# Vision tower on one core: patch sums of the second image half moved behind the first half's value sums, its mean in a product of its own

## Chip, cores, metric

One NeuronCore of a Trainium2 chip. The metric is the device time of one launch in microseconds (us). The kernel before has a median of 334.91 us over 3 runs (334.71 to 335.78).

## What is computed

A small vision tower on 64 images of 3 x 84 x 84, all in float32: a tokenizer, then two layers of delta-rule attention with a gated feed-forward, then a feed-forward with block-wise 4-bit rounding of inputs and weights. The change lies in the tokenizer, which gives 4 window tokens and 1 class token of 256 channels for each image. Cut to what matters:

```python
pe = conv(pixel_values, conv_w, stride 14)            # 6 x 6 patches of 14 x 14, 256 channels
grid = pe in windows of 3 x 3                         # 4 windows an image, 9 patches each
red = mean of the 9 patches                           # one query vector for a window
win = the 9 patches
q = _ln(red) @ la_wq;   k_, v_ = _ln(win) @ la_wkv     # 8 heads of 32
attn = softmax(q . k_ * scale over the 9)
agg = sum over the 9 of attn * v_
local_out = red + agg @ la_proj_w + la_proj_b
```

The kernel carries a mean-free form: the convolution weights are centred over the channels, so its `red` lacks the channel mean. That mean is a linear function of the pixels and is added back where `local_out` is formed.

## The kernel before

**Tiling.** A window is a column. The 256 windows (4 for each of 64 images) are two halves of 128, the "image halves" hf 0 and 1. The pixels lie in six groups g of 384 columns (3 patches x 128 windows): groups 0 to 2 are the first half, 3 to 5 the second. Each group is 5 chunks of 120 pixel rows (`xg`, in the tile `big`). The convolution `conv(g, c)` (L1131) makes patches of 128 channels in PSUM, ScalarE copies them to `pecT` (L336), and keys and values are products of `pecT` with the weights, two patches in a unit `un`; units 0 to 4 are the first half, 5 to 9 the second.

**Order.** Each engine runs its own list, written out by hand, and waits on semaphores (the names in `S[...]`), so an instruction that waits holds all that is behind it on its engine.

- GpSimd (L261 on): `patch_sum(g)` adds the three patches of a group into `xs[:, hf]`, 8 additions of 120 x 640 a half (L280); `square_sum(g)` adds the squares of the two channel chunks (L287). The order is patch sums 0 to 2, square sums 0 to 5, patch sums 3 to 5. Behind them GpSimd waits for `gag_mm`, which comes at about 125 us.
- TensorE (L1114 on): `keys(un)` (L1175), `value(un)` (L1189), `gathered(un)` (L1202), which adds a unit's weighted values into a PSUM sum and raises `acc`; `red_mean` (L1211), which gets the channel mean of all 256 windows from `xs` into PSUM bank 3, 10 products of 256 columns as the profile counts them; `project(hf)` (L1226), the output projection; `stat(hf)` (L1163).
- VectorE (L578 on): `scores(un)` (L698 multiplies the keys in PSUM with the query, L701 reduces), `softmax_a` and `softmax_b` (L711 to L728, small operations of 128 x 72, five of them with two inputs in SBUF), `values(un)` (L747 multiplies values in PSUM with the weights of the softmax, L750 adds the pair in SBUF), `bias_mean(hf)` (L762 adds the mean in PSUM and a bias to `redc`, L764 adds a number to it, both into `redb`), `local(hf)` (L772), which adds `redb` to the projection.
- Between these VectorE rounds the weights of the last feed-forward, `weights(piece, part)`: part 0 finds block scales (L593 to L597), part 1 scales them (L604 to L607), part 2 rounds by adding and subtracting a large number (L613, L614), part 3 scales back (L620). The weight tile is 128 x 704.

**What waits for what around the change.** `gathered(un)` needs `values(un)` from VectorE (`vsum`); `value(8)` needs `values(5)`, whose PSUM bank it takes; `project(0)` needs `bias_mean(0)` and (1) (`redb` at 8) and ScalarE's copy of the sum; `bias_mean` needs `red_mean`; `local(1)` needs `project(1)`; L898 behind it needs ScalarE's group statistics.

The functions that the change touches:

Of the kernel before, what the change touches and what calls it, by code (L numbers as in the profile page):

```python
# [5 lines left out]
ALU = mybir.AluOpType  # L6
# [5 lines left out]
P = 128  # L12
C = 256
# [10 lines left out]
KC, KP = 5, 120  # L24
# [4 lines left out]
HALVES = 2  # L29
# [29 lines left out]
def build(nc, xp, cw_d, vec_d, wt_d, wl_d, wf_d, cst_d, out):  # L59
    ctx = ExitStack()  # L60
    with ctx:
# [11 lines left out]
        cmean9 = sb("cmean9", [KP, KC])  # L73
# [9 lines left out]
        xs = sb("xs", [KP, HALVES, KC, P])  # L83
# [53 lines left out]
        redb = big[:, 3840:4864].rearrange("p (a k j n) -> p a k j n", a=HALVES, k=2, j=CH)  # L137
# [35 lines left out]
        ps = ctx.enter_context(nc.psum_tensor("ps", [P, 8, 512], F32))  # L173
# [44 lines left out]
        S = {n: ctx.enter_context(nc.semaphore("s_" + n)) for n in (*once.split(), *EACH)}  # L218
# [42 lines left out]
        @blk_.gpsimd  # L261
        def _(pool):
            nc.gpsimd.memset(ones[:, :], 1.0 / C).then_inc(S["ones"], 1)
            nc.gpsimd.memset(h1[:, 2, :], 0.0).then_inc(S["zeros"], 1)

            n = [0]

            def patch_sum(g):

                pool.wait_ge(s_x[g], 16)  # L270
                hf = g // 3
                for a in range(3):
                    new = xg[:, g, :, a * P:(a + 1) * P]
                    first = g % 3 == 0 and a == 1
                    if g % 3 == 0 and a == 0:
                        continue
                    old = xg[:, g, :, 0:P] if first else xs[:, hf]
                    if not first:
                        pool.wait_ge(S["xsum"], n[0])
                    nc.gpsimd.tensor_tensor(xs[:, hf], old, new, ALU.add).then_inc(S["xsum"], 1)  # L280
                    n[0] += 1

            def square_sum(g):

                pool.wait_ge(S["squared"], 2 * g + 2)
                cols = slice(g % 3 * GRP, (g % 3 + 1) * GRP)
                nc.gpsimd.tensor_tensor(sq[:, 0, cols], sq[:, 0, cols], sq[:, 1, cols], ALU.add  # L287
                                        ).then_inc(S["sqsum"], 1)

            for g in range(3):  # L290
                patch_sum(g)
            for g in range(6):
                square_sum(g)
            for g in range(3, 6):
                patch_sum(g)

            pool.wait_ge(S["gag_mm"], 1)
            nc.gpsimd.memset(act[0:64, FC - 1, :], 0.0).then_inc(S["zeros"], 1)
            for l in range(LAYERS):

                pool.wait_ge(S["lwa"], EACH["lwa"] * l + 16)
                if l:
                    pool.wait_ge(S["bt_mm"], l)
                nc.gpsimd.tensor_copy(wbx[:, :, :, :].rearrange("p c h d -> p (c h) d"),
                                      wb.rearrange("p c h -> p (c h)").unsqueeze(2).broadcast_to([P, CH * H, DH])
                                      ).then_inc(S["wbx"], 1)
                if l == 0:
                    pool.wait_ge(S["m0"], 2)
                    pool.wait_ge(S["x"], 2)
                    nc.gpsimd.tensor_tensor(hT0[:, :, :], hT0[:, :, :], m0[:, :].unsqueeze(1).broadcast_to([P, CH, NT]),  # L310
                                            ALU.add).then_inc(S["h0"], 1)
# [267 lines left out]
        def _(dve):  # L579
# [52 lines left out]
            def weights(piece, part):  # L632

                src = wf[:, piece * INTER:(piece + 1) * INTER]
                if part == 0:
                    if piece == 0:
                        dve.wait_ge(S["ffnw"], 16)
                    quant_scale(src)
                elif part == 1:
                    quant_step(src)  # L640
                elif part == 2:
                    quant_near(src)
                else:
                    quant_back(src, "wq")
# [87 lines left out]
            def values(un):  # L732

                hf, uu = divmod(un, 5)
                n = min(2, NP_ - 2 * uu)
                dve.wait_ge(S["v_mm1"], un + 1)
                if un == 0:
                    dve.wait_ge(S["xsum"], 8)
                if un >= 3:
                    dve.wait_ge(S["acc"], un - 2)  # L740
                w = sc[:, hf, 2 * uu:2 * uu + n, :].unsqueeze(3).broadcast_to([P, n, H, DH])
                src = ps[:, un % 3, 0:n * C].rearrange("p (n h d) -> p n h d", n=n, h=H)
                if n == 1:
                    v.tensor_tensor(vsum[:, un % 3, :].rearrange("p (h d) -> p h d", h=H), src[:, 0], w[:, 0], ALU.mult
                                    ).then_inc(S["vsum"], 1)
                else:
                    v.tensor_tensor(vpr[:, un % 2].rearrange("p n (h d) -> p n h d", h=H), src, w, ALU.mult  # L747
                                    ).then_inc(S["vprod"], 1)
                    dve.wait_ge(S["vprod"], 4 * hf + uu + 1)
                    v.tensor_tensor(vsum[:, un % 3, :], vpr[:, un % 2, 0, :], vpr[:, un % 2, 1, :], ALU.add  # L750
                                    ).then_inc(S["vsum"], 1)

            def bias_mean(hf):

                dve.wait_ge(S["mean_mm"], 1)
                dve.wait_ge(S["vmean"], 2)
                if hf == 0:
                    dve.wait_ge(S["conv"], 6)
                    dve.wait_ge(S["xsum"], 8)
                cols = slice(hf * P, (hf + 1) * P)  # L760
                for j in range(CH):
                    v.scalar_tensor_tensor(redb[:, hf, 0, j, :], redc[:, j, cols], vec[:, V_LPB + j:V_LPB + j + 1],  # L762
                                           ps[:, 3, cols], ALU.add, ALU.add).then_inc(S["redb"], 1)
                    v.tensor_scalar(redb[:, hf, 1, j, :], redc[:, j, cols], vcn[:, 1, j:j + 1], None, ALU.add  # L764
                                    ).then_inc(S["redb"], 1)

            def local(hf):

                b = 3 + hf
                dve.wait_ge(S["proj_mm"], hf + 1)  # L770
                dve.wait_ge(S["redb"], 4 * hf + 4)
                v.tensor_tensor(lc[:, :, :, hf * P:(hf + 1) * P],  # L772
                                ps[:, b, :].rearrange("p (k j n) -> p k j n", k=2, j=CH), redb[:, hf], ALU.add
                                ).then_inc(S["loc"], 1)
# [96 lines left out]
            values(3)  # L871
            values(4)
            scores(5)
            weights(2, 0)
            scores(6)
            bias_mean(0)
            bias_mean(1)
            scores(7)
            local(0)
            weights(2, 1)  # L880
            scores(8)
            scores(9)
            softmax_a(1)
# [2 lines left out]
            values(6)  # L886
            for un in range(7, 10):
                values(un)
            local(1)

            dve.wait_ge(S["rsg"], 2)
            dve.wait_ge(S["gsc_mm"], 2)
# [205 lines left out]
            for p in range(3):  # L1098
                n = P if p < 2 else 64
# [7 lines left out]
            for p in range(3):  # L1107
                n = P if p < 2 else 64
# [6 lines left out]
        def _(pe):  # L1115
            mm = nc.tensor.matmul
# [86 lines left out]
                              start=False, stop=(uu == 4 and c == CH - 1))  # L1203
                last.then_inc(S["acc"], 1)

            def red_mean():
                pe.wait_ge(S["xsum"], 16)
                pe.wait_ge(S["cmean9"], 1)
                pe.wait_ge(S["copied"], 12)
                for k in range(KC):  # L1210
                    last = mm(ps[:, 3, 0:C].rearrange("p (a n) -> p a n", a=HALVES),  # L1211
                              cmean9[:, k:k + 1].broadcast_to([KP, P]), xs[:, :, k, :], start=(k == 0), stop=(k == KC - 1))
                last.then_inc(S["mean_mm"], 1)

            def project(hf):
                b = 3 + hf
                if hf:
                    pe.wait_ge(S["k_free"], 9)
                else:
                    pe.wait_ge(S["redb"], 8)  # L1220
                    pe.wait_ge(S["wcen"], 1)
                pe.wait_ge(S["aggT"], 2 * hf + 2)
                for k, w in ((0, tw(T_PR)), (1, prc)):
                    for j in range(CH):
                        for c in range(CH):
                            last = mm(ps[:, b, k * C + j * P:k * C + (j + 1) * P], w[:, c, j * P:(j + 1) * P], aggT[:, c, :],  # L1226
                                      start=(c == 0), stop=(c == CH - 1))
                last.then_inc(S["proj_mm"], 1)
# [128 lines left out]
            keys(5)  # L1357
            gathered(3)
            keys(6)
            red_mean()  # L1360
            gathered(4)
            keys(7)
            project(0)
# [5 lines left out]
            value(8)  # L1369
            gathered(5)  # L1370
            value(9)
            for un in range(6, 10):
                gathered(un)
            group_scores(0)
# [358 lines left out]
```

## Time and profile before

| | us |
|---|---|
| median of 3 runs (lowest, highest) | 334.91 (334.71, 335.78) |
| the profiled execution, its own time | 336.37 |
| its span, first to last instruction | 334.6 |
| around the span | 1.8 |
| PE busy, DVE busy, ACT busy, POOL busy | 286.7, 210.7, 101.4, 36.6 |

PE is TensorE's matmul side, PEld its weight loads, DVE is VectorE, ACT ScalarE, POOL GpSimd. Times in the trace are from the start of the span. The granted clock is the share of full speed that TensorE was given: 1.00 is 2.4 GHz and 0.50 is 1.2 GHz. PE's busy share of 86% is a mean over the span: it holds stretches in which PE waits and stretches in which it is slow.

### The profile page before, as it was taken

How to read it: one execution, taken by the hardware profiler on the slowest of the kernel's cores; microseconds unless marked ns; L12 is line 12 of the kernel's file. 1: busy time of each engine (PE TensorE's matmuls, PEld its weight loads, DVE VectorE, ACT ScalarE, POOL GpSimd, SP SyncE). 2: the span in 40 equal slices, each digit the busy share in tenths (PEclk: the TensorE clock that was granted, in tenths of full speed). 3: DMA queues.
4: the chain of work that ended last, by engine and by line, in shares of the span. 5: the costliest groups of instructions: out<-in, count | busy, mean ns of one | idle time of the engine just before them, and what ended most of it. 6: DMA issues, size and time to landing. Idle time of an engine off the chain costs nothing.

```text
span 334.6 us, 9652 instructions
## 1 busy us (share of the span) xinstructions
PE 286.7 (86%) x4372; PEld 215.1 (64%) x4372; DVE 210.7 (63%) x408; ACT 101.4 (30%) x206; POOL 36.6 (11%) x32
## 2 busy tenths in 40 slices
PE   0799999997699999957799998976889998698984
PEld 0466677786598987736787765745877674465452
DVE  2056879989877345773673378673672262598892
ACT  1022301320010126873215433665224422403120
POOL 0673100239500003000000000000000000000000
PEclk9999999999599999996967999995795999699999
DMA  8999990000000000000000206000000000000001
GB/s 179 263 228 337 270 398 38 2 0 0 0 2 0 3 0 1 2 2 2 2 4 14 115 0 230 39 0 4 2 3 2 2 0 0 0 3 0 0 0 39
DMA packets 2666, 18.29 MB, mean 55 GB/s; under 512 B 457, under 2 KB 777, under 8 KB 1873
## 3 DMA queue, kind: packets, MB, share of 16 engines
q1 hardware_dynamic: 2641, 17.93, 17.9%
q8 instruction: 19, 0.31, 0.4%
q14 instruction: 6, 0.05, 0.0%
HBM read 17.60 MB, written 0.33 MB: 54 GB/s over the span
## 4 chain that ended last, share of the span: by engine, by line
PE 66%; DVE 19%; ACT 9%; DMA 3%; issue 2%; SPq 0%; DVEq 0%; ACTq 0%
PE ps L1131 13%; PE ps L1422 11%; PE ps L1175 4%; PE ps L1285 4%; PE ps L1504 3%; PE ps L1628 3%; DMA big<-in_patches 3%; PE ps L1189 2%; PE ps L1495 2%; PE ps L1594 2%; PE ps L1514 2%; PE ps L1121 2%; ACT wl L493 2%; PE ps L1543 2%; DVE big L1002 2%
## 5 line engine op out<-in xcount | busy, mean ns | idle before, releaser
L1131 PE MATMUL ps<-big,cwb 120*128 120x384 f32 x120 | 43.7, 518 | 10.4 <-DMA big<-in_patches 10.4
L1131 PEld LDWEIGHTS ps<-big,cwb 120*128 120x128 f32 x120 | 23.9, 203 | 25.7 <-issue 13.3
L1422 PE MATMUL ps<-xT,wl 128*128 128x320 f32 x88 | 24.5, 434 | 0.7 <-ACT wguT L360 0.5
L280 POOL TENSOR_TENSOR xs<-xs,big 120x640 f32<-120x640 f32 x14 | 23.2, 1658 | 4.2 <-DMA big<-in_patches 3.1
L1495 PE MATMUL ps<-wt,big 32*32 32x32 f32 x1280 | 16.1, 208 | 8.2 <-DVE wt L977 5.0
L1422 PEld LDWEIGHTS ps<-xT,wl 128*128 128x128 f32 x88 | 16.6, 190 | 7.8 <-ACT wguT L360 0.7
L1495 PEld LDWEIGHTS ps<-wt,big 32*32 32x32 f32 x1280 | 14.5, 120 | 10.2 <-DVE wt L977 5.7
L999 DVE COPY_PREDICATED wt<-cst,ps 128x320 f32<-128x320 int32 x16 | 8.1, 504 | 19.0 <-PE ps L1504 19.0
L336 ACT COPY pecT<-ps 128x384 f32<-128x384 f32 x12 | 5.7, 478 | 46.6 <-PE ps L1131 46.6
L1504 PE MATMUL ps<-wt,big 32*32 32x32 f32 x1280 | 15.5, 210 | 5.1 <-ACT wt L501 4.0
L1175 PE MATMUL ps<-wt,pecT 128*128 128x256 f32 x72 | 18.8, 410 | 0.0
L1285 PE MATMUL ps<-cst,ones 128*128 128x320 f32 x54 | 18.2, 487 | 0.0
L1504 PEld LDWEIGHTS ps<-wt,big 32*32 32x32 f32 x1280 | 14.4, 121 | 5.6 <-ACT wt L501 4.3
L661 DVE TENSOR_REDUCE part<-pecT 128x128 f32<-128x384 f32 x12 | 7.1, 593 | 16.2 <-ACT pecT L336 16.1
L1189 PE MATMUL ps<-wt,pecT 128*128 128x256 f32 x72 | 16.6, 380 | 0.1
L1628 PE MATMUL ps<-wguT,pecT 128*128 128x352 f32 (+1 forms) x48 | 14.9, 464 | 1.6 <-ACT pecT L545 1.6
L1175 PEld LDWEIGHTS ps<-wt,pecT 128*128 128x128 f32 x72 | 14.4, 206 | 2.6
L1053 DVE TENSOR_TENSOR cwb<-ps,cwb 128x320 f32<-128x320 f32 (+1 forms) x12 | 5.9, 490 | 15.2 <-ACT cwb L318 9.2
L1189 PEld LDWEIGHTS ps<-wt,pecT 128*128 128x128 f32 x72 | 13.4, 190 | 2.4 <-DVE big L750 0.5
L1285 PEld LDWEIGHTS ps<-cst,ones 128*128 128x128 f32 x54 | 11.3, 217 | 4.7 <-issue 1.9
L501 ACT COPY wt<-ps 128x320 f32<-128x320 f32 x16 | 6.6, 422 | 22.8 <-PE ps L1495 22.8
L1594 PE MATMUL ps<-big,wl 128*128 128x320 f32 x48 | 13.4, 434 | 0.0
(267 smaller groups left out, 532.8 us busy)
## 6 DMA issues: line engine op xcount, KB each, us to landing
big<-in_patches SPq DMA_DIRECT2D x6, 900.0 KB, 20.0
wl<-in_layers SPq DMA_DIRECT2D x2, 2176.0 KB, 25.6
wf<-in_ffn SPq DMA_DIRECT2D x1, 2112.0 KB, 26.8
wl<-in_layers SPq DMA_DIRECT2D x2, 1040.0 KB, 22.0
wt<-in_tok SPq DMA_DIRECT2D x1, 1536.0 KB, 39.3
wt<-in_tok SPq DMA_DIRECT2D x1, 768.0 KB, 14.1
cwb<-in_conv SPq DMA_DIRECT2D x1, 600.0 KB, 5.1
cst<-in_constants SPq DMA_DIRECT2D x1, 320.0 KB, 38.5
```

The costliest lines, as they stand in the source:

```text
L280: nc.gpsimd.tensor_tensor(xs[:, hf], old, new, ALU.add).then_inc(S["xsum"], 1)
L661: step(v.tensor_reduce(part[:, min(g % 3, 1), c, :], pecT[:, c, g * GRP:(g + 1) * GRP].rearrange("p (t n) -> p n t", t=3), AX.X, ALU.add))
L999: v.copy_predicated(tc_[:, g, :], m.unsqueeze(1).broadcast_to([P, NB, 32]), bank32(6 + b, slice(0, P))).then_inc(S["tp"], 1)
L1131: last = mm(ps[:, i % 4, 0:GRP], cwc[:, k, c * P:(c + 1) * P], xg[:, g, k, :], start=(k == 0), stop=(k == KC - 1))
L1175: last = mm(ps[:, 4 + un % 2, t * C:(t + 1) * C], pecT[:, c, i * P:(i + 1) * P], wkv[:, c, 0:C], start=(c == 0), stop=(c == CH - 1))
L1189: last = mm(ps[:, un % 3, t * C:(t + 1) * C], pecT[:, c, i * P:(i + 1) * P], wkv[:, c, C:2 * C], start=(c == 0), stop=(c == CH - 1))
L1285: mm(ps[:, bank, 0:NT], ones[:, :], cst[:, 0:NT], start=True, stop=True)
L1422: last = mm(ps[:, bank, 0:NT], w(c, j), x[:, c, :], start=(c == 0), stop=(c == CH - 1))
L1495: last = mm(ps[r, 4 + b, 32 * k:32 * k + 32], apm[r, NB * b + k, own], tc_[r, NB * b + k, :], start=True, stop=True)
L1504: last = mm(ps[r, 6 + b, 32 * k:32 * k + 32], ttc[r, NB * b + k, :], yc[r, NB * b + k, :], start=True, stop=True)
L1594: last = mm(ps[:, 6 + j, 0:NT], wd[:, i, j * P:(j + 1) * P], act[:, i, :], start=(i == 0), stop=(i == FC - 1))
L1628: last = mm(ps[0:n, b + w, 0:352], xqT[:, c, P * p:P * p + n], wguT[:, c, 352 * w:352 * w + 352], start=(c == 0), stop=(c == CH - 1))
```

## The change

GpSimd waits for `acc` at 5, the end of the first half's value sums, before it starts on the patch sums of the second half. The mean is made in two products, one for each half, both in columns 0 to 127 of bank 3; the second one comes behind `value(9)` and waits until `local(0)` has read that bank. `project(0)` waits for the first half's four `redb` operations alone. On VectorE `bias_mean(1)` and `weights(2, 0)` go behind the last values, and `weights(2, 1)` behind `local(1)`.

```diff
@@ -291,6 +291,7 @@
                 patch_sum(g)
             for g in range(6):
                 square_sum(g)
+            pool.wait_ge(S["acc"], 5)
             for g in range(3, 6):
                 patch_sum(g)
 
@@ -752,7 +753,7 @@
 
             def bias_mean(hf):
 
-                dve.wait_ge(S["mean_mm"], 1)
+                dve.wait_ge(S["mean_mm"], hf + 1)
                 dve.wait_ge(S["vmean"], 2)
                 if hf == 0:
                     dve.wait_ge(S["conv"], 6)
@@ -760,7 +761,7 @@
                 cols = slice(hf * P, (hf + 1) * P)
                 for j in range(CH):
                     v.scalar_tensor_tensor(redb[:, hf, 0, j, :], redc[:, j, cols], vec[:, V_LPB + j:V_LPB + j + 1],
-                                           ps[:, 3, cols], ALU.add, ALU.add).then_inc(S["redb"], 1)
+                                           ps[:, 3, 0:P], ALU.add, ALU.add).then_inc(S["redb"], 1)
                     v.tensor_scalar(redb[:, hf, 1, j, :], redc[:, j, cols], vcn[:, 1, j:j + 1], None, ALU.add
                                     ).then_inc(S["redb"], 1)
 
@@ -871,13 +872,10 @@
             values(3)
             values(4)
             scores(5)
-            weights(2, 0)
             scores(6)
             bias_mean(0)
-            bias_mean(1)
             scores(7)
             local(0)
-            weights(2, 1)
             scores(8)
             scores(9)
             softmax_a(1)
@@ -886,7 +884,10 @@
             values(6)
             for un in range(7, 10):
                 values(un)
+            bias_mean(1)
+            weights(2, 0)
             local(1)
+            weights(2, 1)
 
             dve.wait_ge(S["rsg"], 2)
             dve.wait_ge(S["gsc_mm"], 2)
@@ -1203,13 +1204,16 @@
                               start=False, stop=(uu == 4 and c == CH - 1))
                 last.then_inc(S["acc"], 1)
 
-            def red_mean():
-                pe.wait_ge(S["xsum"], 16)
+            def red_mean(hf):
+                pe.wait_ge(S["xsum"], 8 * hf + 8)
                 pe.wait_ge(S["cmean9"], 1)
-                pe.wait_ge(S["copied"], 12)
+                if hf:
+                    pe.wait_ge(S["loc"], 1)
+                else:
+                    pe.wait_ge(S["copied"], 12)
                 for k in range(KC):
-                    last = mm(ps[:, 3, 0:C].rearrange("p (a n) -> p a n", a=HALVES),
-                              cmean9[:, k:k + 1].broadcast_to([KP, P]), xs[:, :, k, :], start=(k == 0), stop=(k == KC - 1))
+                    last = mm(ps[:, 3, 0:P], cmean9[:, k:k + 1].broadcast_to([KP, P]), xs[:, hf, k, :], start=(k == 0),
+                              stop=(k == KC - 1))
                 last.then_inc(S["mean_mm"], 1)
 
             def project(hf):
@@ -1217,7 +1221,7 @@
                 if hf:
                     pe.wait_ge(S["k_free"], 9)
                 else:
-                    pe.wait_ge(S["redb"], 8)
+                    pe.wait_ge(S["redb"], 4)
                     pe.wait_ge(S["wcen"], 1)
                 pe.wait_ge(S["aggT"], 2 * hf + 2)
                 for k, w in ((0, tw(T_PR)), (1, prc)):
@@ -1357,7 +1361,7 @@
             keys(5)
             gathered(3)
             keys(6)
-            red_mean()
+            red_mean(0)
             gathered(4)
             keys(7)
             project(0)
@@ -1369,6 +1373,7 @@
             value(8)
             gathered(5)
             value(9)
+            red_mean(1)
             for un in range(6, 10):
                 gathered(un)
             group_scores(0)
```

## Rows read from the trace of the kernel before

**Rows 1.** The page, span in 40 slices of 8.4 us: granted clock in tenths.
```profile
PEclk9999999999599999996967999995795999699999
```

**Rows 2.** Timeline of POOL, 70 to 90 us: start, us, engine, line, operation, tiles, count.
```profile
74.93 13.07 POOL L280 TENSOR_TENSOR xs<-xs,big 120x640 f32<-120x640 f32 x7
```

**Rows 3.** Chain of waits, 77 to 95 us: start, us, what.
```profile
78.50 2.16 DVE qa L613
...
82.83 2.11 DVE wf L620
...
85.69 0.93 DVE big L750
86.66 1.22 PE ps L1202 x4
87.88 3.41 PE ps L1175 x8
91.29 2.46 PE ps L1211 x10
```

**Rows 4.** Windows: PE, PEld, DVE, ACT, POOL busy, then granted clock.
```profile
81.80:84.90 3.10, 0.06 (x1) 0.00 (x0) 3.06 (x2) 0.00 (x0) 2.88 (x3) 1.00 0.00 0
86.60:91.70 5.10, 5.04 (x14) 4.24 (x15) 3.61 (x9) 0.00 (x0) 1.40 (x1) 0.50 0.00 0
```

**Rows 5.** Timeline of DVE, 40 to 77 us: rounding and pair sums with and without POOL.
```profile
40.85 0.89 DVE L620 TENSOR_TENSOR wf<-qa,qs 128x704 f32<-128x704 f32 x1
...
73.49 1.64 DVE L750 TENSOR_TENSOR big<-big 128x256 f32<-128x256 f32 x1
...
76.32 0.49 DVE L690 TENSOR_TENSOR prod<-q_sb,kqb 128x256 f32<-128x256 f32 x1
```

**Rows 6.** Timelines of DVE and POOL: other operations side by side.
```profile
21.64 1.22 DVE L780 TENSOR_TENSOR vcn<-vec,vmean 128x8 f32<-128x8 f32 x1
29.25 0.97 DVE L668 TENSOR_SCALAR part<-part 128x256 f32<-128x256 f32 x1
...
21.31 4.76 POOL L280 TENSOR_TENSOR xs<-xs,big 120x640 f32<-120x640 f32 x3 [1.86 <-DMA big<-in_patches]
...
28.97 1.09 POOL L287 TENSOR_TENSOR sq<-sq 128x384 f32<-128x384 f32 x1 [1.94 <-ACT sq L329]
...
79.97 2.07 POOL L280 TENSOR_TENSOR xs<-xs,big 120x640 f32<-120x640 f32 x1
```

**Rows 7.** Chain of waits, 95 to 112 us.
```profile
95.93 1.93 PE ps L1226 x16
...
102.43 0.70 DVE sc L701
...
104.07 0.24 DVE sc L711
...
107.29 0.43 DVE big L750
...
107.77 1.99 PE ps L1189 x8
...
111.50 1.78 PE ps L1202 x16
```

**Rows 8.** DVE from 88 us: timeline, and busy time in one window.
```profile
94.11 0.28 DVE L764 TENSOR_SCALAR big<-redc,vcn 128x128 f32<-128x128 f32 x1
...
116.16 0.69 DVE L772 TENSOR_TENSOR big<-ps,big 128x512 f32<-128x512 f32 x1 [3.68 <-PE ps L1226]
120.78 0.19 DVE L898 TENSOR_TENSOR gs<-ps,rsg 128x32 f32<-128x32 f32 x1 [3.93 <-ACT rsg L318]
...
88.20:90.20 2.00, 1.74 (x5) 0.50 0.00 0
```

**Rows 9.** Timeline of PE, 196 to 290 us: two of its idle times.
```profile
204.71 1.32 PE L1121 MATMUL ps<-cwb,ones 128*128 128x320 f32 x4 [1.60 <-ACT cwb L452]
...
287.29 1.54 PE L1608 MATMUL ps<-cst,hT 128*128 128x128 f32 x6 [2.94 <-DVE hT L1082]
```

## The prediction

> **What bounds the kernel now.** The slices of the page come first [rows 1]: TensorE's granted clock is full up to one slice of "5", the eleventh (83.7 to 92.0 us), in the middle of the token stage where the change works. Then GpSimd's timeline there [rows 2]: of its eight second-half patch sums the last seven run back to back from 74.93 to 88.00. Then the chain of waits from 77 us [rows 3]: from 78.50 to 86.62 it goes through VectorE alone, three pieces of weight rounding (L613, L614, L620) of 2.1 to 2.2 us each, values(3) and its pair sum (L750), and at 86.66 TensorE starts gathered(3), which had waited for them. The windows [rows 4] show what TensorE did: nothing from 81.8 on, and then 5.1 us of work at half clock, 1.2 in place of 2.4 GHz. Three things thus cost time here: slow rounding, an idle TensorE, and the clock that fell in the idle time.
>
> Why the rounding is slow is read from its twins [rows 5]. L620 on the first weights, with GpSimd idle, took 0.89; a 256-element L750 is 0.43 at its plain length (the pair sum at 107.29 [rows 7]) but 1.64 at 73.49, where the patch sums begin. Small ones are hit as hard [rows 6]: an addition of 8 elements (L780) took 1.22 us and ended at 22.86, like the first of three patch sums (21.31 and a third of 4.76); a one-input multiplication of SBUF (L668) took 0.97 beside a square sum. And the patch sum of 79.97 took 2.07 in place of 1.59: L613 ended at 80.66 [rows 3] and it ran 1.4 more. So the two take turns, by whole instructions. No operation with PSUM as a source, and no reduction, is among the stretched ones.
>
> **The change part by part, in the profiled execution's frame** (span 334.60, its time 336.37; 1.46 above the median of 334.91, so the sum is taken as a difference and laid on the median).
>
> 1. The sums leave 73.3 to 88.0. The three rounding pieces took 6.5 us from 78.4 to 84.9 and become 3 x 0.92 (0.89 and a gap) = 2.78: 3.76 saved. L750 at 85.69 goes from 0.93 to 0.43 (0.5), the small excess of L690 and one L750 is 0.1. The 1.64 of the early L750 saves nothing: query(1) behind it waits for TensorE anyway. Together 4.36: gathered(3) at 82.30. TensorE still idles about 0.6 before it.
> 2. The idle time is then too short for the clock to fall. gathered(3) 1.22 and keys(6) 3.41 [rows 3] at full clock are half: 2.3 saved.
> 3. red_mean goes from 10 products of 256 columns (2.46) to 10 of 128. A product of 128 columns is 0.12 (project, 16 in 1.93 [rows 7]): 1.2, saved 1.26. Sum so far 7.92: the first half's value sums (acc at 5) end at 86.28 instead of 94.20.
> 4. Here the new wait opens and the eight sums start, at about 86.32. Queued behind the wait on GpSimd are only they and, far off, work that waits for gag_mm (125 us). At this moment VectorE is in bias_mean(0): keys(6) ends at 84.61, scores(6) is two operations of 0.70 [rows 7], then L762, about as long as L764's 0.28 [rows 8], so the first L764 starts at 86.3 too: a tie. L764 is of L668's kind, so I let it be held: first by sum 1, to about 88.0, the second by sum 2, to 88.0 + 1.40 + 0.14 = 89.54. project(0) needs both (redb at 4) and would be ready at 88.0 behind keys(7): 1.55 given back. TensorE's lead is 6.34.
> 5. The scores and local(0) read PSUM or reduce and keep their old lengths, so L711, at 104.07 before, starts at 97.73. Sum 3 ends at 90.94 and five more at 4.76/3 = 1.59 [rows 6] end at 98.9. L711 (two SBUF inputs) waits for that and ends at 99.03, not 97.97: 1.06 lost, and value(8), which waits for values(5) just behind, loses it too. The lead is 5.28.
> 6. red_mean(1) adds 1.2 between value(9) and gathered(6), where TensorE is the bound: the sixteen products of gathered(6) to (9) run back to back before [rows 7] and the VectorE operations between them wait for TensorE. Its input is ready 7 us earlier (98.9 against 106). The lead is **4.1**.
> 7. Moved work is hidden. bias_mean(1) (four operations of about 0.28) and weights(2,0) (1.74 busy in the window) [rows 8] come after values(9), before local(1), where VectorE idles 3.68 now: 2.9 together, 0.8 spare. If that cover fails, each us goes straight to local(1) and the end. weights(2,1), three pieces of at most 0.9, follows local(1), where it idles 3.93. No DMA and no SP queue entry moves; stages behind 131 us start 4.1 earlier on data that is long there.
>
> **Sum: 334.91 - 4.1 = 330.8.** Two costs the trace doesn't show in this place. A 72-element softmax operation beside a patch sum: from below 0.06 (L690, 0.49 against 0.43, met only the end of a sum), from above one full sum, 1.6, each; the nearest in kind is L780, small and held to the end of the sum, so I take the full hold. The bound from above on the whole is not five holds but the end of the last sum: nothing is held after 98.9. If the L764 pair slips in ahead of GpSimd, the lead before the softmax is 7.92, L711 starts at 96.1, it is held by sum 7 and L714 by sum 8, and values(5) ends at 102.4 again. So steps 4 and 5 together cost 2.6 either way; without any hold they cost 0.
>
> A rule is to be weighed here. By the row L690 (0.49 beside a running sum against 0.43 alone) one could take sharing to be cheap and price the softmax at 5 x 0.06 = 0.3; the 8-element row says a full hold. The Trainium skill (SBUF — State Buffer, section "SBUF: two separate sides") has it that the shared pair of ports is an exclusive lock, held for the whole instruction, for VectorE operations in a two-port mode or with two SBUF inputs. It speaks against this change, since the softmax is made of such operations. By the cheap reading the end would be 334.91 - 6.34 + 0.3 + 1.2 = 330.1, with L764 still held, by the rule 330.8; the 1.22 of L780 agrees with the rule.
>
> **Rivals.**
> - **No second collision** (neither L764 nor the softmax is held): 334.91 - 7.92 + 1.2 = 328.2. For: L690. Against: L780, L668. 0.10.
> - **The clock falls at the wait before value(8).** In the forecast TensorE waits 1.1 us there (and 1.55 before project(0)); if the L764 pair slips in, it waits 2.6 at once. A wait of 1.60 left the clock full; one of 2.94, shortly behind another, had it half [rows 9], slice 35 in [rows 1]. A half stretch like the one now (5.1 us of work in it [rows 4], about 6.8 long by steps 84.9 to 91.7) costs 3.4: 334.2. 0.15.
> - **Slower**: the same place, but the clock stays low as in slices 28 and 29 [rows 1] (5 and 7), some 13 us. The dense TensorE work to 116 us then loses 6.5: 334.91 - 4.1 + 6.5 = 337.3. It decides from about 2.9 us of waiting on. 0.05.
> - **The sums aren't the brake**: the rounding is slow for some other reason and stays so; then only red_mean's shape changes, 2 x 1.2 against 2.46, and the time is 334.9. Against it stand six stretched rows, each with a GpSimd instruction beside it. 0.03.
>
> **How the numbers follow.** Forecast 0.67, its own range 329.5 to 332.3 (half a us for the tie, one for where the clock's later half stretches fall). The range 328.4 to 334.0 takes in most of the first rival and the lower part of the second. About 0.3% (1 us) is what a measurement can tell: faster is the forecast, the first rival and part of the second (0.85); same is the rest of the second and the last (0.10); slower 0.05.
>
> **What would show it.** Right: L613, L614 and L620 of the second weights at 0.9; gathered(3) near 82.3; no half clock around 85 to 92; patch sums from about 86.3 to 99; one L764 or softmax operation of over 1 us; L1211 twice, 1.2 each; local(1) still waiting for project(1), not VectorE. Wrong: patch sums that end past 102, softmax operations all at 0.24 beside running sums, or a "5" in the slices from 92 to 117 us.

## The result and the profile after

The changed kernel has a median of 332.83 us (12 runs, 332.17 to 335.15) against 334.69 (12 runs, 332.81 to 336.95) for the one before; the ratio is 0.9944, with a 95% interval of 0.9917 to 0.9970. It is faster by 1.9 us; the time lies inside the range given, but above the forecast's own range of 329.5 to 332.3, and the forecast gain was 4.1. In a second set of runs (e3 below) the ratio was 0.9927 (0.9898 to 0.9956), 2.4 us. Medians here are of all executions, ratios of the fast ones alone against the kernel before in the same session, so a ratio is the safer figure where two sessions are compared.

The page's own rows of the profiled execution (332.94 us) show the slice that had been slow, the eleventh, at full clock now; the rows answer to [rows 1].

```profile
span 331.2 us, 9674 instructions
...
PEclk9999999999999999965978999995895999599999
```

The chain of waits of the changed kernel, 77 to 104 us, answers to [rows 3, 7]. Lines of the changed file stand one to five lines lower (L614 is the old L613, L765 the old L764, L712 the old L711).

```profile
78.24 0.81 DVE qa L614
...
80.01 0.90 DVE wf L621
...
81.66 0.44 DVE big L751
...
82.14 0.71 PE ps L1203 x4
82.85 1.74 PE ps L1176 x8
...
86.48 1.37 DVE big L765
87.85 0.26 DVE big L763
88.10 1.36 DVE big L765
89.51 2.05 PE ps L1230 x16
...
97.70 1.60 DVE sc L712
99.33 0.24 DVE sc L715
...
102.77 1.99 PE ps L1190 x8
```

All steps of the prediction stand there in a row: the three rounding pieces at 0.9, gathered(3) at 82.14 (forecast 82.30), keys(6) at 1.74, then the two L765 that wait for a patch sum each, project(0) at 89.51 (forecast 89.6), one softmax operation held for 1.6, and value(8) at 102.77 (forecast 102.5). The patch sums run from 86.22 to 99.20 (forecast 86.3 to 98.9), in GpSimd's timeline, where 86 to 99 us answers to [rows 2]:

```profile
86.22 1.54 POOL L280 TENSOR_TENSOR xs<-big 120x640 f32<-120x640 f32 x1 [13.01 <-PE ps L1203]
87.84 11.36 POOL L280 TENSOR_TENSOR xs<-xs,big 120x640 f32<-120x640 f32 x7
```

The timeline of VectorE, which answers to [rows 8], shows local(1) still waiting for TensorE with 1.12 to spare, and L899 with 2.01:

```profile
111.02 0.19 DVE L598 TENSOR_SCALAR qs<-qs 128x44 f32<-128x44 f32 x1
112.33 0.69 DVE L773 TENSOR_TENSOR big<-ps,big 128x512 f32<-128x512 f32 x1 [1.12 <-PE ps L1230]
...
116.95 0.19 DVE L899 TENSOR_TENSOR gs<-ps,rsg 128x32 f32<-128x32 f32 x1 [2.01 <-ACT rsg L319]
```

So the token stage did nearly what was said, and the first projection of layer 0 starts at 126.33 instead of 130.15. The span of this pair of profiles followed, 331.2 for 334.6, but the medians are only 1.9 apart: the execution profiled before was 1.7 above its median, the one here 0.1. The experiments ask where the rest went.

The measure used below divides an execution in three, by TensorE's timeline: from the first convolution product to query(1), the products that make the second half's queries, which no version here but one touches; from query(1) to the first projection of layer 0, the **stage**; and from there to the last instruction, the **layers**. A **record** is one matmul as the trace counts it; a float32 product of the source is two records.

### The profile page after: what moved, and what is told of

Same layout as the page of the kernel before. It is cut to its first block, busy times and chain, and to the rows that moved or that the text cites. A ratio compares the mean times of both kernels' runs of the same rounds, so it can differ in the third digit from the quotient of the medians.

```text
span 331.2 us, 9674 instructions
## 1 busy us (share of the span) xinstructions
PE 283.9 (86%) x4382; PEld 212.6 (64%) x4382; DVE 208.8 (63%) x408; ACT 101.1 (31%) x206; POOL 35.0 (11%) x32
## 4 chain that ended last, share of the span: by engine, by line
PE 64%; DVE 20%; ACT 10%; issue 3%; DMA 3%; SPq 0%; DVEq 0%; ACTq 0%
PE ps L1132 13%; PE ps L1427 11%; PE ps L1289 4%; PE ps L1176 3%; PE ps L1509 3%; PE ps L1633 3%; DMA big<-in_patches 3%; PE ps L1500 2%; PE ps L1190 2%; PE ps L1599 2%; PE ps L1122 2%; PE ps L1519 2%; ACT wl L494 2%; PE ps L1548 2%; DVE big L1003 2%
## 5 line engine op out<-in xcount | busy, mean ns | idle before, releaser
L1500 PE MATMUL ps<-wt,big 32*32 32x32 f32 x1280 | 17.0, 212 | 9.6 <-DVE wt L978 5.0
L1500 PEld LDWEIGHTS ps<-wt,big 32*32 32x32 f32 x1280 | 15.1, 123 | 11.7 <-DVE wt L978 5.7
L280 POOL TENSOR_TENSOR xs<-xs,big 120x640 f32<-120x640 f32 x14 | 21.5, 1536 | 4.2 <-DMA big<-in_patches 3.1
L1509 PE MATMUL ps<-wt,big 32*32 32x32 f32 x1280 | 15.9, 213 | 3.6 <-ACT wt L502 2.3
L1190 PE MATMUL ps<-wt,pecT 128*128 128x256 f32 x72 | 16.6, 380 | 1.4 <-DVE big L751 1.4
L1509 PEld LDWEIGHTS ps<-wt,big 32*32 32x32 f32 x1280 | 15.0, 126 | 4.1 <-ACT wt L502 2.6
L1176 PE MATMUL ps<-wt,pecT 128*128 128x256 f32 x72 | 17.0, 381 | 0.0
L1190 PEld LDWEIGHTS ps<-wt,pecT 128*128 128x128 f32 x72 | 13.4, 190 | 3.8 <-DVE big L751 1.8
L1176 PEld LDWEIGHTS ps<-wt,pecT 128*128 128x128 f32 x72 | 13.3, 190 | 2.3
```

The source lines that it names most:

```text
L1176: last = mm(ps[:, 4 + un % 2, t * C:(t + 1) * C], pecT[:, c, i * P:(i + 1) * P], wkv[:, c, 0:C], start=(c == 0), stop=(c == CH - 1))
L1190: last = mm(ps[:, un % 3, t * C:(t + 1) * C], pecT[:, c, i * P:(i + 1) * P], wkv[:, c, C:2 * C], start=(c == 0), stop=(c == CH - 1))
L1500: last = mm(ps[r, 4 + b, 32 * k:32 * k + 32], apm[r, NB * b + k, own], tc_[r, NB * b + k, :], start=True, stop=True)
L1509: last = mm(ps[r, 6 + b, 32 * k:32 * k + 32], ttc[r, NB * b + k, :], yc[r, NB * b + k, :], start=True, stop=True)
```

## Experiments

Theory A: the clock falls before [rows 4] in only part of the executions, so that step 2 was priced from the worst. Against it B: it falls always and the loss is elsewhere. When the layers turned out to differ between versions that leave them alone, three more followed: C, the layers' time depends on the moment at which they start; D, it is chance, and has nothing to do with the start; E, TensorE stops at fixed places of its instruction stream.

**e1, the kernel before, unchanged.**

> The kernel before, unchanged, to see what its executions share. Theory A (the clock falls in only part of the executions of before): its times spread over some 4 us again, the profiled one has a wait before gathered(3) of 4.8 us and VectorE's rounding at 2.1 us as always, but its granted clock in the stretch from 85 to 92 us is full or half only briefly in some executions, so acc at 5 comes at 92 to 94 us and not always at 94.2. Theory B (the clock falls there always, and the loss is elsewhere): acc at 5 at 94.2 again, and a spread no wider than that of the changed kernel.

Median 335.19. The profiled execution waits the same 4.80 for gathered(3), but the clock was half for only 3.4 us (85.9 to 89.3) against 6.8 (85.0 to 91.8) in the first profile. The wait, and the windows of the second profile, to be set beside [rows 4]:

```profile
85.44 0.85 PE L1202 MATMUL ps<-cst,big 128*128 128x128 f32 x4 [4.80 <-DVE big L750]
...
81.00:85.00 4.00, 0.00 (x0) 0.00 (x0) 3.90 (x4) 0.00 (x0) 3.92 (x2) 1.00 0.00 0
...
86.00:89.00 3.00, 3.00 (x9) 2.45 (x8) 2.69 (x6) 0.00 (x0) 0.79 (x1) 0.50 0.00 0
89.00:93.00 4.00, 4.00 (x21) 3.53 (x20) 2.56 (x8) 0.63 (x2) 0.00 (x0) 0.96 0.00 0
```

The stage took 54.69 against 55.49. It also fell in g1 below (stage 55.01), the third profile without a filler, after a wait of 3.79, so neither theory as put is right: always a fall, of unequal worth. How often the short and the long fall come is not shown by three profiles.

**e2, a filler in the wait for gathered(3) of the kernel before.** `keep_clock(bank, n)` makes n products whose results nobody reads; the kernel uses them to keep TensorE at work.

```diff
             keys(5)
+            pe.wait_ge(S["copied"], 12)
+            keep_clock(3, 7)
             gathered(3)
```

> Before, with seven clock-keeping products in the wait for gathered(3), nothing else. They end before the wait does. Theory A: the spread of before shrinks, its slow executions go, and the median falls by the share of executions in which the clock fell, 0.5 to 1.5 us. Theory B: the clock fell always, so all executions gain 2.3 us or more (ratio 0.993).

The clock did not fall and the stage took 53.22, 1.5 to 2.3 us less than in those three profiles. But the median was 335.37, ratio 1.0006 (0.9974 to 1.0038): nothing gained. Its layers took 206.46 us against 204.45 and 203.97, though their code is the same. This is the first sign that the stage's gain can be lost behind it.

**e3, the changed kernel, unchanged.**

> The changed kernel, unchanged. Both theories: 332.8 us, token stage over (first projection of layer 0) at 126.3 us; patch sums 86.2 to 99.2; L765 twice at 1.4 us and L712 once at 1.6.

332.72, ratio 0.9927 (0.9898 to 0.9956). Its stage is 51.80 (51.82 in the first profile), its layers 206.75 (204.87). The stage is the same in both profiles; the layers differ by 1.9 us.

**e4, the held operations moved and the sums started sooner.**

```diff
-            pool.wait_ge(S["acc"], 5)
+            pool.wait_ge(S["vsum"], 4)
...
+            def bias_centred():
...
+                for hf in range(HALVES):
+                    for j in range(CH):
+                        v.tensor_scalar(redb[:, hf, 1, j, :], redc[:, j, hf * P:(hf + 1) * P], vcn[:, 1, j:j + 1], None,
+                                        ALU.add).then_inc(S["redb"], 1)
...
             values(1)
+            bias_centred()
             query(1)
```

> The changed kernel, but the four one-input operations of the bias (L765) stand before query(1), in VectorE's wait for TensorE, and the patch sums wait for vsum at 4 (82.1 us) rather than acc at 5 (86.2). If the holds at L765 and L712 are what steps 4 and 5 cost, both go: project(0) follows keys(7) at once (1.6 us), the sums end at about 95 before the softmax begins at 96 (1.4 us), and the time is 3.0 us below the changed kernel's, 329.8 us. If holds move on instead (the sums run into the softmax after all, or slow the values), it gains under 1.5 us.

Measured 329.60, ratio 0.9846 (0.9794 to 0.9898), from six executions. Expected was 329.8. VectorE's and TensorE's timelines show both holds gone: the four additions lie in VectorE's wait for TensorE at query(1), and value(8) follows value(7) without a pause, 32 products in one piece.

```profile
73.82 0.87 DVE L770 TENSOR_SCALAR big<-redc,vcn 128x128 f32<-128x128 f32 x4
...
95.92 0.23 DVE L712 TENSOR_TENSOR sc<-sc,rk 128x72 f32<-128x72 f32 x1
...
94.23 7.40 PE L1196 MATMUL ps<-wt,pecT 128*128 128x256 f32 x32
```

The sums ran from 82.30 to 95.30, 0.6 us ahead of the softmax. The stage is 48.55, 3.3 below the changed kernel's, so the two holds of steps 4 and 5 cost about what the prediction gave them.

**f1, f2, f3: delays ahead of layer 0.** One clock-keeping product more or less just ahead of the layers shifts them in time, and by two records, and changes nothing else. f1 adds four to e2, f2 three and f3 six to the changed kernel. By theory D the whole delay is paid (337.6, 334.4, 336.1), by C less or more (336.4, 335.5, 336.2).

```diff
             norm_sum(ps[:, 5, NW:NT], sqx[:, :, NW:NT], ones[:, :]).then_inc(S["x_var"], 1)
-            keep_clock(4, 2)
+            keep_clock(4, 6)   # f1; 5 in f2, 8 in f3
```

> Before with the filler in the wait for gathered(3) (335.4 us), and four more clock-keeping products just ahead of layer 0, which delay it by 2.26 us. Theory C (the layers' time depends on when layer 0 starts relative to the moments at which the chip moves the clock, and the filler version starts it at a bad time: its layers took 206.5 us against 204.2 in the two looks at before): only 0.8 to 1.3 us of the delay are seen, 336.4 us, layers near 205. Theory D (the layers' time is chance and has nothing to do with the start): the whole delay is paid, 337.6 us.

> The changed kernel with three more clock-keeping products ahead of layer 0, a delay of 1.7 us. Theory C: it pays more than the delay, since layer 0 then starts as in the version with the filler: layers near 206.5 in all executions, 335.5 us. Theory D: 332.75 + 1.7 = 334.4 us.

> The changed kernel with six more products ahead of layer 0, a delay of 3.4 us: layer 0 starts as late as in the kernel before. Theory C: layers as in the changed kernel, 205 to 206, so 336.2 us. Theory D: 336.1 us. Taken with the run before, theory C has a step of only 0.7 us from three products to six, theory D one of 1.7.

Medians 338.48, 334.36, 335.97. Only f1 and f2 tell the two theories apart. f2 falls where D had it. f1's median lies above both, 3.1 above e2's; but the two were run in different sessions, and by their ratios (1.0075, 1.0044 to 1.0106, against e2's 1.0006) f1 is 2.3 us longer, which is D's 2.26 of delay. Both are where D has them; the intervals, over 1 us to either side, do not exclude C outright. What varies inside the layers is in the timelines of TensorE. Inside the first solve of layer 0 the products stand in blocks of 80 or 160, and some blocks are cut by an idle time that waits for nothing the profile shows ("issue"), a **stop**. Before, this stretch has one:

```profile
149.35 1.09 PE L1495 MATMUL ps<-wt,big 32*32 32x32 f32 x80 [1.07 <-DVE wt L977]
152.56 1.96 PE L1504 MATMUL ps<-wt,big 32*32 32x32 f32 x129 [2.12 <-ACT wt L501]
154.87 0.65 PE L1504 MATMUL ps<-wt,big 32*32 32x32 f32 x31 [0.34 <-issue]
```

The changed kernel has three, and the first stands in a block that had been whole:

```profile
145.55 1.18 PE L1500 MATMUL ps<-wt,big 32*32 32x32 f32 x71 [0.67 <-DVE wt L978]
147.43 0.37 PE L1500 MATMUL ps<-wt,big 32*32 32x32 f32 x9 [0.70 <-issue]
148.75 1.82 PE L1509 MATMUL ps<-wt,big 32*32 32x32 f32 x118 [0.96 <-ACT wt L502]
151.29 0.79 PE L1509 MATMUL ps<-wt,big 32*32 32x32 f32 x42 [0.73 <-issue]
152.38 2.36 PE L1500 MATMUL ps<-wt,big 32*32 32x32 f32 x160 [0.30 <-issue]
```

With the six more records of f2 the pieces behind the first two stops have 15 and 48 in place of 9 and 42, and with the twelve more of f3 21 and 54:

```profile
147.14 0.43 PE L1500 MATMUL ps<-wt,big 32*32 32x32 f32 x15 [0.31 <-issue]
151.01 0.86 PE L1509 MATMUL ps<-wt,big 32*32 32x32 f32 x48 [0.37 <-issue]
```

```profile
150.41 0.54 PE L1500 MATMUL ps<-wt,big 32*32 32x32 f32 x21 [0.68 <-issue]
154.55 0.96 PE L1509 MATMUL ps<-wt,big 32*32 32x32 f32 x54 [0.98 <-issue]
```

The first of the two fences is f2, the second f3. These stops sit at fixed places of TensorE's instruction stream: every record put in ahead of them moves the code past them by one. This is theory E. Counted over the whole kernel it is plainer still: in the 14 profiles here the stops of 0.15 us or more stand behind 843, 971 (or 970), 2183, 2690, 2818 (or 2817) and 4030 records, at no other place but at the start of a block of 160 right behind such a stop, while the first solve begins behind 682 to 728 records. Not every profile has all of them. The kernel before had its first place just behind the 80 products, in a wait of 2.12 us for ScalarE, where it costs nothing; the change's ten more records pulled it inside the block. A part of a stop is then taken back behind it: that wait is 0.96 in the changed kernel.

The stops meet something else in the trace. The page has a queue with 19 packets of instructions, here as the changed kernel's page gives it:

```profile
q8 instruction: 19, 0.31, 0.4%
```

Each packet is 16384 bytes and takes 0.9 to 1.6 us by the trace. In the changed kernel packets start at 144.8 and 148.7 and the stops end at 147.43 and 151.29. All 52 stops of 0.15 us or more at the six places, in all profiles, end 2.3 to 3.0 us behind the start of such a packet. Before, a packet starts at 148.6 and would be done with, by the same count, at 150.9 to 151.6, while TensorE waits for ScalarE until 152.56. This speaks for TensorE waiting for its own instructions; no experiment moved a packet.

**f4, the rounding piece back in its old places.**

```diff
             scores(5)
+            weights(2, 0)
             scores(6)
...
             local(0)
+            weights(2, 1)
             scores(8)
...
             bias_mean(1)
-            weights(2, 0)
             local(1)
-            weights(2, 1)
```

> The changed kernel with weights(2,0) and weights(2,1) back in their old places, behind scores(5) and local(0). The block scales delay scores(6) by 0.9 but not the value sums. weights(2,1) has three operations that contend for GpSimd's port (L605, L607, L608), now beside running patch sums: each is held up to 1.5 us, VectorE ends them at about 97 us and not at 94.4, so scores(8) starts 2 us late, but then the sums are nearly over and L712 is not held (1.4 back). Net 0.5 to 1.5 us slower than the changed kernel: 333.3 to 334.2. If the moved piece costs nothing where it was, 332.8.

335.01, 2.3 us above the changed kernel by the medians and 2.1 by the ratios (0.9989, 0.9960 to 1.0017), more than expected. The three operations were held as said (0.88, 0.53 and 0.53 without a sum beside them), and the softmax operation, expected free, still lost 0.5:

```profile
92.01 1.16 DVE L605 TENSOR_TENSOR qa<-wf,qs 128x704 f32<-128x704 f32 x1
93.20 1.75 DVE L607 TENSOR_SCALAR qa<-qa 128x704 int32<-128x704 int32 x1
94.99 1.75 DVE L608 TENSOR_SCALAR qa<-qa 128x704 f32<-128x704 f32 x1
...
99.13 0.72 DVE L712 TENSOR_TENSOR sc<-sc,rk 128x72 f32<-128x72 f32 x1
```

On top, the wait before value(8) was now 2.23 and the clock was half from 104.4 to 107.8, behind it: the second rival's mechanism. TensorE's timeline (value(8) took 1.99 in the changed kernel) and the window:

```profile
103.32 2.79 PE L1190 MATMUL ps<-wt,pecT 128*128 128x256 f32 x8 [2.23 <-DVE big L751]
...
104.40:107.80 3.40, 3.40 (x12) 2.87 (x11) 0.95 (x2) 0.00 (x0) 0.00 (x0) 0.50 0.00 0
```

So the moved rounding is a part of the change that pays by itself.

**g1, the kernel before with ten more records.**

```diff
             keys(5)
+            pe.wait_ge(S["copied"], 12)
+            for _ in range(5):
+                mm(ps[:, 3, 0:1], ones[:, :], ones[:, 0:1], start=True, stop=True)
             gathered(3)
```

> The kernel before with five one-column products in TensorE's 4.8 us wait for gathered(3), as many instructions ahead of the layers as the change adds. Theory E (TensorE's stream stops for its own instructions at fixed places of the stream; the change's ten more product records move such a place from a wait into the middle of the 80 products of the solve's first level): the token stage stays as in before, layer 0 shows its 80 products of L1495 cut into 71 or 70 and the rest by an issue hole of 0.4 to 1.0 us, a second hole near product 118 of L1504, and the layers take 1.0 to 1.5 us longer: 336.1 us. Theory D (the layers' time is chance): 335.0 us and holes as in before.

The stops came where theory E put them, as in the changed kernel, though this program has nothing of the change:

```profile
148.02 1.18 PE L1498 MATMUL ps<-wt,big 32*32 32x32 f32 x71 [1.07 <-DVE wt L977]
149.90 0.34 PE L1498 MATMUL ps<-wt,big 32*32 32x32 f32 x9 [0.70 <-issue]
151.22 1.81 PE L1507 MATMUL ps<-wt,big 32*32 32x32 f32 x119 [0.99 <-ACT wt L501]
153.77 0.79 PE L1507 MATMUL ps<-wt,big 32*32 32x32 f32 x41 [0.73 <-issue]
```

The places are thus shown to follow the count of records. The price is not: the time was 335.57, ratio 1.0027 (0.9996 to 1.0058), an interval that holds both no change and the 1.0 to 1.5 us expected, and the layers took 204.39 in the profile, as before (204.45, 203.97), with 3.4 us of stops in place of 1.0 and 0.6.

**g2 and h1, five clock-keeping products less.** g2 is e4, h1 the changed kernel, both without the five `keep_clock` products ahead of layer 0, ten records.

```diff
-            keep_clock(4, 2)
             pe.wait_ge(S["k_free"], 10)
...
-            keep_clock(4, 1)
             pe.wait_ge(S["gag"], 2)
...
             norm_sum(ps[:, 5, NW:NT], sqx[:, :, NW:NT], ones[:, :]).then_inc(S["x_var"], 1)
-            keep_clock(4, 2)
```

> The early-gate version without its five clock-keeping products ahead of layer 0, which takes the ten records back that the change added. Theory E: the 80 products run whole again and the holes in the layers fall from 2.1 to about 1 us: 328.6 us, unless the clock falls for want of the keeping products, which would show as a half stretch before layer 0 and cost up to 2 us. Theory D: 329.7.

> The changed kernel without its five clock-keeping products ahead of layer 0. Theory E (issue holes at fixed places of TensorE's stream): the holes of the first solve level go, as in the early-gate version, the layers take 203 to 204 us instead of 205 to 206.7 and the time is 331.3 us; the token stage is as in the changed kernel. If the gain of the early-gate version came from the products themselves, or was chance, 332.5.

g2: 327.92, ratio 0.9808 (0.9763 to 0.9853), no stop in either layer's solve, layers 203.33. h1: 331.62, ratio 0.9890 (0.9853 to 0.9928), 1.1 us below the changed kernel of e3, its stage 51.80 as before, layers 204.29, the block of 80 whole:

```profile
145.32 1.18 PE L1497 MATMUL ps<-wt,big 32*32 32x32 f32 x80 [1.08 <-DVE wt L978]
148.52 1.71 PE L1506 MATMUL ps<-wt,big 32*32 32x32 f32 x111 [2.02 <-ACT wt L502]
```

The clock stayed full up to the layers without the products. Both pairs go the way of theory E (1.7 us from e4 to g2, 1.1 from e3 to h1), but the intervals of the ratios overlap in each pair (0.9763 to 0.9853 and 0.9794 to 0.9898; 0.9853 to 0.9928 and 0.9898 to 0.9956), and g2 has six executions, h1 seven.

**g3, products in the wait for the first patches.**

```diff
+            pe.wait_ge(S["ones"], 1)
+            for _ in range(18):
+                mm(ps[:, 7, 0:P], ones[:, :], ones[:, :], start=True, stop=True)
             pe.wait_ge(S["cwc"], 3)
             conv(0, 0)
```

> The early-gate version with 18 products of 128 columns in TensorE's wait for the first patches (0.9 to 10.3 us). In the six looks so far the clock first rose at 13.7 to 16.7 us and the time from the first convolution product to query(1) was 62.9 to 64.3, longer the later it rose. If that is the clock, the convolution starts at the full clock, this stretch takes 61.5 or less, or what the patches' landing allows, and the time falls by 1 to 2 us, with the holes in the solve at new places.

332.97, 3.4 slower than e4. The first twenty convolution products took 6.69 us instead of 9.54, as expected, but the chain then waited for the last feed-forward's weights, which VectorE's list has ahead of its share of the query, and the clock fell from 39.3 to 46.1:

```profile
4.08 29.84 DMA wf<-in_ffn
...
39.29 0.43 DVE redc L672
...
39.75 0.42 ACT redq L343
...
40.22 1.01 PE ps L1149 x4
```

A gain ahead of a DMA's landing turned into a wait and a clock fall behind it. Another order of VectorE's list was not tried here.

All profiled executions in one table. Stops are the issue times of 0.15 us or more in the two layers' solves, summed; half clock is the time within the layers at which TensorE was granted 0.50.

| us | stage | layers | stops | half clock in the layers | median |
|---|---|---|---|---|---|
| before, first profile; e1 | 55.49; 54.69 | 204.45; 203.97 | 1.0; 0.6 | 44.8; 41.4 | 334.69; 335.19 |
| e2, before with filler | 53.22 | 206.46 | 2.2 | 51.7 | 335.37 |
| f1, e2 with delay | 55.15 | 207.73 | 4.6 | 51.8 | 338.48 |
| g1, before with ten records | 55.01 | 204.39 | 3.4 | 41.9 | 335.57 |
| changed; e3 | 51.82; 51.80 | 204.87; 206.75 | 2.9; 3.4 | 45.1; 51.6 | 332.83; 332.72 |
| f2, changed with delay | 53.22 | 205.71 | 3.0 | 51.9 | 334.36 |
| f3, changed with longer delay | 54.81 | 205.36 | 3.7 | 48.5 | 335.97 |
| f4, rounding back | 54.23 | 205.31 | 2.2 | 51.9 | 335.01 |
| h1, changed, five products less | 51.80 | 204.29 | 0.4 | 48.3 | 331.62 |
| e4, early gate | 48.55 | 204.31 | 2.1 | 41.4 | 329.60 |
| g2, early gate, five products less | 48.54 | 203.33 | 0.0 | 41.4 | 327.92 |
| g3, early gate, warm start | 48.56 | 206.67 | 1.8 | 44.9 | 332.97 |

The layers without their stops lie between 201.0 and 204.9, so a stop is not simply added to the time. Two things vary together in this table. Where the half-clock time is nearly equal the stops can be priced: before against changed, e1 against g1, g2 against e4, and h1 against f3 differ by 1.9, 2.8, 2.1 and 3.3 us of stops, and by 0.4, 0.4, 1.0 and 1.1 us of layers. And the half-clock time goes with the length: the changed kernel's two profiles have 45.1 and 51.6 us of it, nearly the same stops, and layers of 204.87 and 206.75. It differs between executions of one program, so a single profile of the layers can be 2 us off for this alone.

## Why the prediction was wrong in size

**Right, step by step.** Steps 1 to 3 gave the lead at gathered(4): 4.37 up to gathered(3) (forecast 4.36), 3.54 from there (forecast 2.3 + 1.26), both from the two first profiles. Step 4 cost 1.76 (forecast 1.55), and the tie between L764 and the sums fell as assumed, which was luck as to the place; the prediction had the same total for the other outcome. Steps 5 and 6 cost 2.48 together (forecast 1.06 + 1.2). The stage gained 3.67 for 4.1 forecast. Step 7's cover for the moved work held, with 1.1 to spare. The exclusive turns of VectorE and GpSimd, which the prediction took from an 8-element row, held for a 72-element operation: 1.60 for 0.24, where the cheap reading priced all five at 0.3. This agrees with the rule that the prediction cites from the Trainium skill (SBUF — State Buffer, section "SBUF: two separate sides"). The first rival (no second collision) is refuted by the same row, the second (a clock fall before value(8)) did not happen after a wait of 1.43 and did in f4 after one of 2.23, the third didn't happen, and the fourth is refuted by the rounding at 0.9.

**The step that failed** is the last sentence of step 7, "stages behind 131 us start 4.1 earlier on data that is long there", that is, that the layers would run as before. Step 3 counted the ten more records for their own time (1.2 us for each half) and for nothing else. They also move TensorE's later code past places where its stream stops: 2.9 and 3.4 us of such stops in two profiles of the changed kernel, 1.0 and 0.6 in two of the one before. That ten records alone bring the same stops is shown by g1, and that taking ten away removes nearly all of them by h1. Their price is less sure: 0.4 to 1.1 us by the pairs of like half-clock time, 1.1 between the medians of e3 and h1, and nothing clear of noise in g1.

**A size that was off** is step 2. The 2.3 us for the fallen clock is right for the execution that was profiled, which was 1.46 above the median. With the shorter fall of e1 the stretch from gathered(3) to gathered(4) was 6.12 and in g1 6.45, not 6.93, so steps 2 and 3 together gave 2.7 and 3.1 instead of 3.54, and the whole stage gained 2.9 or 3.2 instead of 3.67. The prediction noticed the 1.46 and laid the difference on the median all the same. Over the three profiles the stage gained 3.2. Less the 0.4 to 1.1 us of the stops that leaves 2.1 to 2.8, against 1.9 and 2.4 measured: 0.4 of the shortfall is step 2, 0.4 steps 4 to 6, and the rest, 1.3 or 0.8, falls to the layers as far as these runs tell. (In step 4 the recorded 1.55 us given back and the lead of 6.34 do not quite agree: 7.92 less 6.34 is 1.58.)

**Open** is what the stops cost in the mean of many executions, why the half-clock time in the layers varies, and what the stops are: that TensorE waits for its own instructions fits their places and the packets, but was not tested.

## What to carry to other kernels

VectorE and GpSimd collided here by whole instructions, so a block of long GpSimd work is placed by what VectorE does beside it. Beside the 1.5 us patch sums, operations that read PSUM and reductions kept their length (L699 and L702 at 0.69), while operations with two SBUF inputs, and the one-input L765, were held to the end of a sum: up to 1.4 us each, however small. A block that is moved out of one crowd should be laid in the gap ahead of the next, so that it ends before the next such operation starts (e4: the sums end at 95.30, the softmax starts at 95.92; 3.1 us for one earlier gate and four operations moved). Price a clock fall from several executions. When a change adds instructions to a stream, search dense stretches far behind it for blocks newly cut by "issue": taking out five cheap products went with 1.1 and 1.7 us less in the two pairs here. The best version, g2, has the ratio 0.9808, from six executions: 6.4 us less than the kernel before.

## What was not expected of the hardware

- A stop of TensorE by nothing shown, 0.16 to 1.2 us, at places fixed in its instruction stream: 9, 15 and 21 records from the end of the same block with 0, 6 and 12 records added ahead, behind 843 records in all three. Each ends 2.3 to 3.0 us behind the start of a 16384-byte instruction packet.
- One program's clock falls for 3.4 us in one execution and 6.8 in another after the same 4.80 us wait.
- The time from the first convolution product to query(1), all TensorE, was 62.9 to 64.3 us in all profiles but g3's, growing with the moment at which the clock first rose (14.2 us: 63.02; 16.7: 64.27). That alone is 1.4 us between executions of one program.
- An operation with one SBUF input and a number for each partition (L765, 128 elements) is held like a two-input one: 1.45 against 0.28.
